# A four-layer graph network on one core: 58 of its edge slots are fetched row by row by SyncE, not gathered by GpSimd

## What is computed

```python
x = _layernorm(x + L0(x))   # L0: h = x @ W.T + b;      out[src] += h[dst]
x = _layernorm(x + L1(x))   # L1: agg[dst] += x[src];   two matmuls, layer norm, relu
x = _layernorm(x + L2(x))   # L2: agg[src] += weight * x[dst];  two matmuls, each with a batch norm
x = _layernorm(x + L3(x))   # L3: attention over the edges of each node, softmax by target node
```

## Time and profile before

| | |
|---|---|
| median of three runs | 6393.77 us |
| span of the profiled execution, first to last instruction | 5360.5 us |
| between that span and the median | 1033.3 us |
| GpSimd (POOL) busy | 3859.6 us, 72% of the span |
| VectorE (DVE) busy | 3591.6 us, 67% |
| TensorE (PE) busy | 3080.4 us, 57% |
| layer 0: first gather starts, last ends | 1060.49 to 2044.87 us |
| layer 1 | 2069.24 to 3053.83 us |
| layer 2 | 3090.60 to 4073.13 us |

### The profile page before, as it was taken

How to read it: one execution, slowest core, us unless ns; L and a number is a source line. 1 busy time by engine, 2 the same in 40 slices (tenths; PEclk the granted TensorE clock), 3 DMA queues, 4 the chain that set the end, 5 groups by cost and what they waited for, 6 DMA issues and landing times. The chain is left out here.

```text
span 5360.5 us, 59783 instructions
## 1 busy us (share of the span) xinstructions
PE 3080.4 (57%) x13425; PEld 2445.6 (46%) x13425; DVE 3591.6 (67%) x11544; ACT 1583.2 (30%) x4870; POOL 3859.6 (72%) x4039
## 2 busy tenths in 40 slices
PE   5777776243333343555555556566567577677676
PEld 4555554133333333444444434444444455555554
DVE  9999998455555555666666645555554777777777
ACT  4222221000000000000000122222223567777776
POOL 7777777777777776777777577777774177777775
PEclk9999988555665565667666777877888888888888
DMA  4222222177777776777777633333332233433432
GB/s 116 79 75 79 79 77 68 30 214 224 221 222 225 221 221 192 213 217 216 215 217 215 175 104 105 105 105 105 105 105 60 71 105 108 112 110 110 112 111 81
DMA packets 307815, 740.55 MB, mean 138 GB/s; under 512 B 88370, under 2 KB 116233, under 8 KB 307480
## 3 DMA queue, kind: packets, MB, share of 16 engines
q0 software_dynamic: 229648, 629.40, 40.5%
q1 hardware_dynamic: 77832, 107.50, 6.5%
HBM read 689.24 MB, written 47.38 MB: 137 GB/s over the span
## 5 line engine op out<-in xcount | busy, mean ns | idle before, releaser
L2081 DVE TENSOR_TENSOR ACC<-ps,ACC 128x256 f32 x2352 | 999.2, 425 | 767.5 <-PE ps L1435 499.7
L852 POOL DMA_INDIRECT ZT<-table,meta_dst x832 | 805.1, 968 | 390.6 <-issue 190.1
L1435 PE MATMUL ps<-ZT_parts,xT_parts 128*128 128x256 f32 x3136 | 698.5, 409 | 515.6 <-DMA ZT_parts<-table,meta_src 271.8
L783 POOL DMA_INDIRECT rec_src<-ZT x784 | 759.4, 969 | 254.9 <-issue 233.1
L852 POOL DMA_INDIRECT ZT<-table,meta_src x784 | 743.9, 949 | 275.4 <-issue 156.3
L852 POOL DMA_INDIRECT ZT_parts<-table,meta_dst x784 | 746.1, 952 | 252.9 <-issue 163.8
L852 POOL DMA_INDIRECT ZT_parts<-table,meta_src x784 | 745.8, 951 | 238.8 <-issue 164.5
L1435 PEld LDWEIGHTS ps<-ZT_parts,xT_parts 128*128 128x128 f32 x3136 | 665.7, 319 | 544.8 <-DMA ZT_parts<-table,meta_src 284.8
L1462 PE MATMUL ps<-ZT,xT 128*128 128x256 f32 x1664 | 517.0, 456 | 184.2 <-DVE X L2405 161.6
L1435 PE MATMUL ps<-ZT,xT 128*128 128x256 f32 x1568 | 501.0, 489 | 141.5 <-DMA ZT<-table,meta_src 141.5
L1435 PEld LDWEIGHTS ps<-ZT,xT 128*128 128x128 f32 x1568 | 398.9, 257 | 247.2 <-DMA ZT<-table,meta_src 161.2
(11 more groups left out here) (450 smaller groups left out, 5485.9 us busy)
## 6 DMA issues: line engine op xcount, KB each, us to landing
ACC<-in_edge_attr SPq DMA_DIRECT2D x108, 256.0 KB
ACC<-in_edge_attr SPq DMA_DIRECT2D x88, 224.0 KB
ZT<-table,meta_dst POOLq DMA_INDIRECT x832
rec_src<-ZT POOLq DMA_INDIRECT x784
ZT_parts<-table,meta_src POOLq DMA_INDIRECT x784
ZT_parts<-table,meta_dst POOLq DMA_INDIRECT x784
ZT<-table,meta_src POOLq DMA_INDIRECT x784
table<-meta_dst SPq DMA_DIRECT2D x24, 512.0 KB
```

The costliest lines, as they stand in the source:

```text
L783: pool.indirect_dma_start(rec_src, bass.IndirectOffsetOnAxis(ap=rec_of[0][:, c:c + 1], axis=0), pay_src[:, c, :], None).then_inc(scattered ...
L852: pool.indirect_dma_start(slot(s), None, rows, bass.IndirectOffsetOnAxis(ap=ids[:, s, 0:1].bitcast(I32), axis=0)).then_inc(gathered[s // G ...
L1435: mm = nc.tensor.matmul(o, chosen, part, start=(i == 0), stop=(i == len(parts) - 1))
L2081: v.tensor_tensor(dst, slot_sum(j), dst, ALU.add).then_inc(sem["added"], 1)
```

## The change

In layers 0 and 1 eighteen slots, and in layer 2 the slots of `range(4, 48, 2)`, 22 of them, are no longer gathered. GpSimd leaves them out (but still waits for `summed` at each). SyncE fetches them: it loads 32 row addresses at a time from SBUF into registers and issues one DMA per row, 128 for a slot, into one of two side buffers in turn. In layers 0 and 1 the buffers are the former `cslot` and `reset` tiles and a row goes as four pieces of 128 floats; in layer 2 they lie in `ZT` and a row goes as 257 contiguous floats. SyncE starts on a slot when the slot before the last one of its own has been summed, and TensorE waits at such a slot for its 128 rows. The stores of the finished pairs are written out between the loads of 32 addresses, at places fixed by `ROW_PACE`, `ROW_AHEAD`, `PARTS_AT` and `STORES_AT`. VectorE works out the addresses in 8 or so small instructions per list (`list_row_slots`). GpSimd writes `slot_no` again after layer 1, since `reset` has been used. Semaphores used to count the steps of the norms are given up for the common chain; the instructions stay.

```diff
+ROW_BINS = [[4 + 5 * i // 2 for i in range(18)], [4 + 5 * i // 2 for i in range(18)], range(4, T - 1, 2)]
+ROW_CHUNK = 32
+ROW_PARTS = P // ROW_CHUNK
+ROW_AHEAD = 10
+ROW_PACE = 9
+PARTS_AT = 92
+STORES_AT = 170
+def row_slot(b):
+    return b * BIN + 2 * (b // CB + 1)
...
 # SyncE
+            def row_chunk(layer, at, part):
+                s, q = ROW_SLOTS[layer][at], at % 2
+                if part == 0 and at < 2:
+                    sp.wait_ge(sem["table_in"], TABLE_IN[layer])
+                    sp.wait_ge(sem["row_known"], layer + 1)
...
+                if part == 0 and at >= 2:
+                    sp.wait_ge(sem["summed"], row_slot_summed(layer, ROW_SLOTS[layer][at - 2]))
+                width = WS if layer < 2 else D
+                _, found = nc.values_load_multi_w_load_instructions(
+                    row_ids[layer % 2][s % CH:s % CH + 1, part * ROW_CHUNK:(part + 1) * ROW_CHUNK],
...
+                for i, first in enumerate(found):
+                    e = part * ROW_CHUNK + i
+                    if layer < 2:
+                        row = flat[bass.ds(first, WS)].rearrange("(a i d) -> a i d", a=1, i=4)
+                        sp.dma_start(row_home(layer, q)[e:e + 1, :, :].bitcast(F32), row).then_inc(rows_in[layer][q], 16)
+                    else:
+                        row = flat[bass.ds(first, D + 1)].rearrange("(a d) -> a d", a=1)
+                        sp.dma_start(row_home(layer, q)[e:e + 1, :], row).then_inc(rows_in[layer][q], 16)
+            def chunks_among(layer, store, first):
+                j = 0
+                for at, s in enumerate(ROW_SLOTS[layer]):
+                    for part in range(ROW_PARTS):
+                        begins = s - ROW_AHEAD - (ROW_PARTS - part) * ROW_PACE
+                        while store is not None and j < NJ and first + j * R <= begins:
+                            store(j)
+                            j += 1
+                        row_chunk(layer, at, part)
...
 # GpSimd, in gather()
+                    if s in ROW_SLOTS[layer]:
+                        continue
...
+            pool.wait_ge(sem["summed"], 2 * SUMS)
+            pool.iota(slot_no[:, :], [[1, SLOTS3]], base=0, channel_multiplier=0,
...
 # TensorE, in slot_sums()
+                    if g * G + j in ROW_SLOTS[layer]:
+                        pe.wait_ge(*rows_landed(layer, g * G + j))
...
 # VectorE
+            def list_row_slots(n):
+                chosen = cols[0:CH, 0:UC]
...
+                for c in range(UC):
+                    names = unit_rows[n][0:CH, c, :, 0]
+                    link(v.tensor_scalar(mine, names, chosen[:, 0:1], None, ALU.mult) if c == 0 else
+                         v.scalar_tensor_tensor(mine, names, chosen[:, c:c + 1], mine, ALU.mult, ALU.add))
```

More of the change, by code:

```diff
@@ L97 @@
 assert NJ == SITERS
+ROW_BINS = [[4 + 5 * i // 2 for i in range(18)], [4 + 5 * i // 2 for i in range(18)], range(4, T - 1, 2)]
[7 more added lines that the diff above has]
+    return b * BIN + 2 * (b // CB + 1)
+ROW_SLOTS = [[row_slot(b) for b in bins] for bins in ROW_BINS] + [[]]
+assert UC == BIN // 2 - 1 and all(s % BIN and s < SLOTS for slots in ROW_SLOTS for s in slots)
 RING_TILE = T - R3
@@ L185, in all_rounds_3, with gathers_in, gathers_until @@
         body(i, i // RG3, i % RG3)
-def ring_uses(layer, n):
-    return sum(len(range(n, GROUPS, RINGS[i])) for i in range(layer) if n < RINGS[i])
+def gathers_in(layer, g):
+    return sum(s not in ROW_SLOTS[layer] for s in range(g * G, g * G + G))
+def gathers_until(layer, g):
+    n = g % RINGS[layer]
+    before = sum(gathers_in(i, h) for i in range(layer) if n < RINGS[i] for h in range(n, GROUPS, RINGS[i]))
+    return before + sum(gathers_in(layer, h) for h in range(n, g + 1, RINGS[layer]))
 def ring_place(layer, g):
@@ L280, in gnn_program @@
         tile_dst = sb("tile_dst", [P, SUMS + 1], I32)
-        reset = sb("reset", [P, SLOTS3])
-        cslot = sb("cslot", [P, SLOTS3])
+        reset, reset_parts = two_names("reset", [P, SLOTS3])
+        cslot, cslot_parts = two_names("cslot", [P, SLOTS3])
         sel_x, sel_x_parts = two_names("sel_x", [P, P])
@@ L409, in gnn_program @@
         meta = [meta_src, meta_dst, meta_src, meta_dst]
+        row_sum = [ewW[:, n * P:(n + 1) * P] for n in range(2)]
+        row_ids = [rows.bitcast(I32) for rows in row_sum]
         value_3 = tile_dst[:, 0:SLOTS3].bitcast(F32)
@@ L412, in gnn_program, with row_home, row_operand @@
         table_at = [flat_dst[:, 400:400 + SUMS], z1[:, 128:128 + SUMS]]
+        def row_home(layer, q):
+            if layer < 2:
+                return (cslot_parts, reset_parts)[q][:, 0:4 * (P + 4)].rearrange("p (i d) -> p i d", i=4)[:, :, 0:P]
+            return ZT[:, q * (D + 1):(q + 1) * (D + 1)]
+        def row_operand(layer, q):
+            if layer < 2:
+                home = row_home(layer, q)
+                return [home[:, 0:2, :], home[:, 2:4, :]]
+            return [row_home(layer, q)[:, 0:D]]
         def job_norms(n):
@@ L486, in gnn_program @@
         scattered2 = [ctx.enter_context(nc.semaphore(f"scattered2_{i}")) for i in range(SG)]
+        rows_in = [[ctx.enter_context(nc.semaphore(f"rows_in{i}_{q}")) for q in range(2)] for i in range(3)]
         attr_in = [ctx.enter_context(nc.semaphore(f"attr_in{i}")) for i in range(AR)]
@@ new lines, in chunks_among @@
+            def chunks_among(layer, store, first):
[7 more added lines that the diff above has]
+                        row_chunk(layer, at, part)
+                if store is not None:
+                    for j in range(j, NJ):
+                        store(j)
@@ L2034, in _ @@
             take_list(0)
+            list_row_slots(0)
             def select(layer, r, k):
@@ L2148, in rows_0 @@
                     ins = v.tensor_tensor(place(acc3, j, i), place(acc3, j, i), x, ALU.add)
-                step0(j, ins)
-                row_stats(0, step0, j, job_norms(0), [place(acc3, j, i) for i in range(len(rows))])
+                link(ins)
+                row_stats(0, j, job_norms(0), [place(acc3, j, i) for i in range(len(rows))])
             def scales_0(j):
-                one_over(0, step0b, j, job_norms(0), in_job(j), j + ROWS[0])
+                one_over(0, j, job_norms(0), in_job(j), j + ROWS[0])
             def parts_0(j):
@@ L2290, in back @@
                 wait(dve, sem["back_used"], b + 1)
-                row_stats(3, back_step, b, norms(3)[:, q], [tile_of(acc3, b, j) for j in range(nt)])
+                row_stats(3, b, norms(3)[:, q], [tile_of(acc3, b, j) for j in range(nt)])
             def rows_2(b, q, nt):
-                one_over(3, back_last, b, norms(3)[:, q], nt, b + (ROWS[2] - 1))
+                one_over(3, b, norms(3)[:, q], nt, b + (ROWS[2] - 1))
             h_step = norm_steps("h_step", 1)
```

93 lines of the change are left out of this document (58 added, 35 removed).

## The result

The changed kernel took 10251.88 us in the median (10245.72 to 10267.62) beside 6391.14 us of the kernel before: a ratio of 1.6042, 95% interval 1.602 to 1.6065. It is slower, as forecast, but by 3861 us where 665 were forecast, and far outside the range.

The account below looks back on a forecast made before the run. GpSimd's gathers bound layers 0 to 2; SyncE would become the bound, adding 221, 130 and 314 us, together 665, taking 6393.8 to about 7060 us. The forecast's own range was 6850 to 7250, the 8-in-10 range 6315 to 7200.

Parts of the forecast that it names:

- What bounds the kernel: Layers 0 to 2: GpSimd's issue of gathers, about 1.256 us each, sets the length; leaving slots out removes 72.8 us.
- SyncE becomes the bound: Layers 0 to 2: SyncE needs 62.4, 59.1 and 58.2 us per slot against 49.0, 49.0 and 38.9 between slots.
- the sum's form: Per layer, SyncE's slot times plus stores and ends: 1204, 1114 and 1296 us, together +665 us.
- The row of layer 2: SyncE's one-row fetch: 0.42 us from start to start, its DMA 0.25 us.
- The step that failed: Layers 0 and 1: a four-piece row priced at 0.42 us like a one-partition DMA, with 0.50 as upper bound.
- Rival D: Layers 0 and 1: four-piece rows cost 0.50 us, 369 us more, 7430 us; chance 0.08, dearer loads included.
- A load of 32 addresses: SyncE's load into registers, four per slot: 2.14, 1.33 and 1.1 us in layers 0, 1 and 2.
- The 1033.3 us around it, which I leave as they are: Time taken to lie outside the 5360.5 us profiled span, added unchanged to reach the median of 6393.8 us.
- What costs nothing: VectorE's address work (3 us, covered), the moved iota and the norms' changed semaphores add no time.
- Rival B's rule: Starting DMAs is small beside the DMA, so SyncE keeps pace and 72.8 us are won: 6321 us; rival's chance 0.31.
- What I said would be seen: Changed profile: SyncE's rows 0.42 us apart, TensorE waiting on side buffers, GpSimd's gathers in bursts with 10 to 20 us waits.
- What would make it worse is a DMA queue that fills up: SyncE's row DMAs: a full queue holding SyncE was named as what would make the time worse; no size given.

Follow-up runs that it names:

- one-piece form: Changed kernel with rows of layers 0 and 1 fetched as one piece instead of four, all 58 slots: 6153.59 us, 1.1456 against the kernel before, in a free set.
- free set: Set of runs in which the unchanged kernel before takes about 5361 us; the changed kernel took 7836.44 us there beside 5372.38, ratio 1.4587.
- held-up: Said of sets or executions in which the unchanged kernel before takes about 6391 us; the changed kernel took 10251.88 us there, ratio 1.6042.
- the kernel without rows: Changed kernel with ROW_BINS empty, so every slot is gathered and address work and the other edits stay: ratio 1.0007 against the kernel before, in a held-up set.

## Why the prediction was wrong

- **What bounds the kernel** was read rightly. GpSimd's gathers set the length of three layers, and one left out gives back about 1.3 us: 43 us for 33 and 56 us for 42 where SyncE keeps up.
- **SyncE becomes the bound** was right, and so were the shape of the profile and the sum's form. In the one-piece form, in a free set, layers 0, 1 and 2 took 1165, 1154 and 1372 us where the sum said 1204, 1114 and 1296, and the whole cost 781 us where it said 665. That the first two come so close is in part luck: a row there took 0.391 us and not 0.42, 67 us less in each layer, and in layer 1 dearer loads took 72 x 0.86 = 62 us of that back.
- **The row of layer 2** was right: 0.405 us against 0.42, its DMA 0.241 against 0.25.
- **The step that failed: "four pieces may cost what 15 partitions do, 0.334, and a row 0.50. I take 0.42, since one partition is the nearest form".** A row in four pieces costs 0.75. Both rows that I took it from, 0.25 and 0.334, are of DMAs with one piece in a partition, so neither could price a second piece, and the bound of 0.50 was no bound. It was the largest single miss, 4608 x (0.75 - 0.42) = 1521 us. Rival D named the pieces, but with the same bound of 0.50, and for their packets. The packets did come, six more for a row (346553 with four pieces less 318905 with one, over 4608 rows, from the profiles' pages), but the cost is in the issue itself, 0.581 us alone as beside gathers.
- **A load of 32 addresses** was taken as 2.14, 1.33 and 1.1 us; it takes 2.2 to 2.4 in every layer. In layer 2 that is 88 x 1.07 = 94 us, and the row, 0.015 us cheaper than taken, gave 42 back: 52 of the 76 us by which the layer ran over. An address beyond the first two costs (2.19 - 0.73) / 30 = 0.05 us in layer 1, which was my upper bound; I had taken 0.02. The Trainium skill, Runtime: NRT & Kernel Launch, section Instruction fetch mechanics, has about 200 ns for each register; the runs disagree for loads from SBUF, 2.2 us for 32 being 69 ns each.
- **"The 1033.3 us around it, which I leave as they are"** was wrong. They don't lie around the span. The profile that I read was of a free execution and the times were of held-up ones, and the two should have made me ask what slows one by 1.19 inside the span. Of the 3861 us this is 1397: in the recorded run the layers are 612, 569 and 680 us longer than in the free one, and the kernel without rows takes some 136 to 145 us longer in each.
- **What costs nothing**: right, 1.0007, in a held-up set.
- **Rival B's rule**, in the Trainium skill, DMA: Bandwidth & Descriptors, section Issuing engines are not separate DMA queues: that starting a DMA is small beside the DMA. For rows of 1 or 2 KB, 128 to a slot, the runs disagree: SyncE's starts, one behind another, set the length of the layers. The same section says that DMAs started by different engines interleave on the same DMA engines; in the eleven-slot run that did no harm, GpSimd's idle time before a gather staying at 0.30 us.
- **What I said would be seen**: rows 0.42 us apart in layer 2, TensorE's waits on the two buffers, GpSimd's gathers in bursts, all there. GpSimd's waits were to be 10 to 20 us. One of 92.75 stands above; in the one-piece form in a free set the longer ones are 5 to 25. "What would make it worse is a DMA queue that fills up": what made it worse was the form of the row, as dear with nothing else running.

Shown, by taking the cause away: the pieces, 1683 us; too many slots too close together, the remaining 781 (with SyncE's earlier start in the same edit). Shown beside each other, but not taken away in this kernel: that gathers hold SyncE up in a held-up set. How much of the 1397 us falls on the pieces was not measured, since the one-piece form never met such a set with all its slots. They aren't needed for it: eleven one-piece slots per layer win 43 us in a free set and cost 945 in a held-up one (7339.3 beside 6394.19), so there 988 us come with the set, 30 for each of 33 slots, where 1397 is 24 for each of 58.

## What to carry to other kernels

What a DMA costs the engine that issues it went here by its form, not by its bytes: 0.21 us became 0.57 at the second piece. Before one is issued thousands of times, its own form has to be timed by itself. Work can be moved to an idle engine as far as that engine's own time per unit fits between two units of the bound one: 58 slots cost 781 us, 42 slots, further apart, won 56. And where the profiled execution and the timed ones differ by a fifth, as here, look for what differs inside the span before the difference is added as a constant.

## What the hardware did that I had not expected

- Issuing the DMA of a row in two to eight pieces takes SyncE 0.567 to 0.627 us, in one piece 0.208, at 1024 and at 2048 B.
- There are two conditions, 5361 and 6391 us for the same program. In the longer one, while GpSimd gathers and up to 10 us beyond, the instructions of TensorE, VectorE, ScalarE and SyncE mostly start 0.7 or 1.4 us apart, register and DMA-issuing steps included. The kernel before, whose bound is GpSimd, loses 19%, the changed one, with thousands of small instructions on SyncE, 31% (10252 against 7836). What sets the condition is open.
- So the same change can be a gain or a loss: eleven one-piece slots per layer give 0.992 in the one and 1.149 in the other.
